# 32-wide attention with the operands of the value product exchanged

## The reference

```python
# layer 0: one shared key and value head
Q = (x @ Wq_w.T + Wq_b).reshape(b, l, NUM_HEADS, HEAD_DIM)
K = x @ Wk_w.T + Wk_b
V = x @ Wv_w.T + Wv_b
scores = jnp.einsum('bqhd,bkd->bhqk', Q, K) * scale
attn = jax.nn.softmax(scores, axis=-1)
out = jnp.einsum('bhqk,bkd->bqhd', attn, V)
# layer 1: keys and values of their own for each head, then an output projection
scores = jnp.einsum('bthd,bshd->bhts', q, k) * softmax_scale
attn = jax.nn.softmax(scores, axis=-1)
ctx = jnp.einsum('bhts,bshd->bthd', attn, v)
```

## Time and profile before

| | |
|---|---|
| median of three runs | 2578.72 us |
| the profiled execution, its time and span | 2575.5 us, 2573.8 us |
| PE busy | 2410.4 us |
| DVE busy | 1743.5 us |
| ACT busy | 1182.5 us |
| 512 weighing records of layer 0, of layer 1 | 116.9 us busy each |

### The profile page before, as it was taken

The page is one execution under the profiler, slowest core; times in us unless marked ns, Lnnn a source line. Parts: engine busy times, 40 slices in busy tenths (PEclk is TensorE's granted clock), DMA queues, the critical chain, the costliest instruction groups (busy, mean ns, idle before and its releaser), DMA issues. The chain is left out here.

```text
span 2573.8 us, 38285 instructions
## 1 busy us (share of the span) xinstructions
PE 2410.4 (94%) x11324; PEld 1771.1 (69%) x11324; DVE 1743.5 (68%) x3696; ACT 1182.5 (46%) x2318; POOL 157.0 (6%) x263
## 2 busy tenths in 40 slices
PE   7899988799999899999996999999999999999679
PEld 5555556677777788555564777777777777776457
DVE  6577877778887654666656666667666666666643
ACT  3477765323333522677723444444444444444221
POOL 0000000100000000000031010101010100000100
PEclk9999999899999999999998999999999999999789
DMA  5622200000000226433102000000000000000101
GB/s 164 196 73 69 71 1 1 1 1 0 0 0 1 83 103 198 112 98 93 41 0 65 2 12 12 16 4 16 4 16 4 16 12 8 12 0 0 43 0 66
DMA packets 71226, 104.10 MB, mean 40 GB/s; under 512 B 14090, under 2 KB 27146, under 8 KB 71018
## 3 DMA queue, kind: packets, MB, share of 16 engines
q1 hardware_dynamic: 71146, 103.08, 13.4%
HBM read 73.16 MB, written 29.88 MB: 40 GB/s over the span
## 5 line engine op out<-in xcount | busy, mean ns | idle before, releaser
L3142 DVE SCALAR_TENSOR_TENSOR x_res<-xa_out_bank,xa_den,x_res 128x512 f32 (+1 forms) x256 | 191.3, 747 | 158.0 <-PE xa_out_bank L2782 158.0
L3051 ACT ACTIVATE xa_pT_hi<-xa_t_bank 128x512 fp32r<-128x512 f32 x256 | 149.5, 597 | 126.0 <-PE xa_t_bank L2919 126.0
L501 DVE TENSOR_REDUCE l1s_mx<-l1s_max_bank 128x1 f32<-128x512 f32 x256 | 156.4, 680 | 68.8 <-PE l1s_max_bank L359 68.8
L3062 ACT ACTIVATE xa_prob<-xa_prob,xa_nmax 128x512 f32<-128x512 f32 x256 | 182.7, 715 | 30.1 <-DVE xa_nmax L3124 30.1
L2782 PE MATMUL xa_out_bank<-xa_o_w,xa_o_hi 128*128 128x512 f32 x512 | 173.9, 421 | 22.3 <-DVE x_res L3142 20.8
L3106 DVE TENSOR_TENSOR xa_pT_lo<-xa_t_bank,xa_pT_hi 128x512 fp32r<-128x512 f32 x256 | 175.6, 686 | 23.1 <-ACT xa_pT_hi L3051 19.0
L501 DVE TENSOR_REDUCE l0s_mx<-l0s_max_bank 128x1 f32<-128x512 f32 x256 | 156.8, 680 | 47.0 <-PE l0s_max_bank L359 46.9
L3124 DVE CUSTOM_DVE_ANT_0 xa_prob<-xa_s_bank,xa_mask_bias 128x512 f32<-128x512 f32 x256 | 171.1, 687 | 20.2 <-PE xa_s_bank L2782 9.6
L2169 DVE SCALAR_TENSOR_TENSOR ffn_yT<-ffn_y,ffn_ysc,ffn_yT 128x512 f32<-128x512 f32 x176 | 129.5, 745 | 46.9 <-PE ffn_y L1915 46.8
L2919 PE MATMUL xa_t_bank<-ident,xa_prob 128*128 128x128 f32 x1024 | 150.6, 275 | 0.0
L2919 PEld LDWEIGHTS xa_t_bank<-ident,xa_prob 128*128 128x128 f32 x1024 | 121.0, 141 | 39.7 <-issue 18.2
(11 more groups left out here) (481 smaller groups left out, 5851.0 us busy)
## 6 DMA issues: line engine op xcount, KB each, us to landing
l0s_q<-l_q SPq DMA_DIRECT2D x96, 128.0 KB, 2.4
l1s_q<-l_q SPq DMA_DIRECT2D x96, 128.0 KB, 3.0
l1s_k<-l_k SPq DMA_DIRECT2D x96, 128.0 KB, 3.1
l0s_k<-l_k SPq DMA_DIRECT2D x96, 64.0 KB, 2.4
x_res<-in_x_dram SPq DMA_DIRECT2D x4, 1024.0 KB, 9.6
l_q<-l_q_hi SPq DMA_DIRECT2D x16, 256.0 KB, 2.6
l_q<-l_q_lo SPq DMA_DIRECT2D x16, 256.0 KB, 3.2
l_q<-l_hi SPq DMA_DIRECT2D x16, 256.0 KB, 2.1
```

The costliest lines, as they stand in the source:

```text
L501: dve.tensor_reduce(self.mx[:, j // QT, j % QT:j % QT + 1], self.max_bank[j % 3][:], AX.X, ALU.max)\
L3051: act.activation(pT_hi[:, kt % (QT - 1), :], t_bank[kt % 2][:], ACT.Copy).then_inc(pT_hi_done, 1)
L3062: act.activation(prob[:, q, :], prob[:, q, :], ACT.Exp, bias=nmax[:, q:q + 1], scale=-1.0, accum_out=den[:, r, 0, q:q + 1]).then_inc(exp_d ...
L3142: dve.scalar_tensor_tensor(xt, out_bank[:], den[:, r, 2, q:q + 1], xt, ALU.mult, ALU.add)\
```

## The change

The two operands of the weighing are exchanged. The probabilities of 128 queries are held (128 columns) and the values with their column of ones are moved (33 columns), one matmul for each key tile, head and query tile: 32 in a pair, where there were 8. The output has queries in partitions, as DVE reads it. ACT's copy, PE's turn, the tile `oT` and the semaphores `oT_ready` and `turned` are gone. Two PSUM banks, before the output's and the turned one's, take the outputs of even and odd pairs. PE waits at the weighing of pair p until DVE has read the output of pair p-2 (`o_read`); DVE's reciprocal waits for the weighing itself. The room that `oT` lent to another weight's scales is a tile of its own.

```diff
         if kt == 0:
             pe.wait_ge(self.v_staged, p + 1)
-            reached(pe, self.oT_ready, p)
+            reached(pe, self.o_read, p - 1)
         pe.wait_ge(self.exp_done, 8 * p + 2 * kt + 2)
         for n in range(2):
-            last = pe.matmul(self.o_bank[self.W * n:self.W * (n + 1), :], self.vs[s % 2][:, kt, n, :],
-                             self.pT[:, n, kt, :], start=(kt == 0), stop=(kt == QT - 1))
+            for q in range(QT):
+                last = pe.matmul(self.o4[s % 2][:, q, n, 0:HD + 1], self.pT[:, n, kt, q * P:(q + 1) * P],
+                                 self.vs[s % 2][:, kt, n, 0:HD + 1],
+                                 start=(kt == 0 and n == 0 and q == 0),
+                                 stop=(kt == QT - 1 and n == 1 and q == QT - 1))
         if kt == QT - 1:
             last.then_inc(self.weighed, 1)
-
-    def turn(self, pe, p):
-
-        pe.wait_ge(self.oT_ready, p + 1)
-        reached(pe, self.o_read, p)
-        for q in range(QT):
-            last = pe.transpose(self.t_bank[:, q * P:(q + 1) * P], self.oT[:, q * P:(q + 1) * P], self.st.ident[:])
-        last.then_inc(self.turned, 1)
...
                 self.score(pe, p, s, k)
-                if k == 4 and not self.early(p, 1):
-                    self.turn(pe, p - 1)
...
-    def take_oT(self, act, p):
-        act.wait_ge(self.weighed, p + 1)
-        reached(act, self.turned, p)
-        act.activation(self.oT[:], self.o_bank[:], ACT.Copy).then_inc(self.oT_ready, 1)
...
-    def invert(self, dve, p):
-        dve.wait_ge(self.turned, p + 1)
-        dve.reciprocal(self.rden[:], self.o4[:, :, :, HD:HD + 1]).then_inc(self.rden_done, 1)
+    def invert(self, dve, p, s):
+        dve.wait_ge(self.weighed, p + 1)
+        reached(dve, self.o_read, p)
+        dve.reciprocal(self.rden[:], self.o4[s % 2][:, :, :, HD:HD + 1]).then_inc(self.rden_done, 1)
...
-        self.o4 = self.t_bank[:].rearrange("p (q n d) -> p q n d", q=QT, n=2)
+        self.o4 = [bank[:].rearrange("p (q n d) -> p q n d", q=QT, n=2) for bank in (self.o_bank, self.t_bank)]
```

More of the change, by code:

```diff
@@ L273, in __init__ @@
             st.sems("maxed", "max_read", "ms_ready", "mrow_turned", "mrow_ready", "scored", "exp_done")
-        self.weighed, self.oT_ready, self.turned, self.o_read, self.max_hi_done, self.rden_done, self.on_done = \
-            st.sems("weighed", "oT_ready", "turned", "o_read", "max_hi_done", "rden_done", "on_done")
+        self.weighed, self.o_read, self.max_hi_done, self.rden_done, self.on_done = st.sems(
+            "weighed", "o_read", "max_hi_done", "rden_done", "on_done")
         self.ks_made, self.vs_cleared, self.vs_made, self.v_staged, self.ms_cleared = \
@@ L290, in __init__ @@
         self.vs = [sb(f"{name}_vs{s}", [P, QT, 2, self.W], F32) for s in range(2)]
-        between("turned")
-        self.oT = sb(f"{name}_oT", [P, S], F32)
+        between("out")
         self.max_bank = [ps(f"{name}_max_bank{g}", [P, S]) for g in range(3)]
@@ L426, in tensor @@
         self.rounds(pe, step)
-        self.turn(pe, self.NP - 1)
     def make_constants(self, pool):
@@ L471, in rows @@
                 .then_inc(self.mrow_ready, 1)
-    def take_oT(self, act, p):
-        act.wait_ge(self.weighed, p + 1)
-        reached(act, self.turned, p)
-        act.activation(self.oT[:], self.o_bank[:], ACT.Copy).then_inc(self.oT_ready, 1)
     def scalar(self, act, beside=None):
         def step(p, s):
-            if not self.early(p, 1):
-                self.take_oT(act, p - 1)
             for k in range(8):
@@ L493, in scalar @@
         self.rounds(act, step)
-        self.take_oT(act, self.NP - 1)
     def reduce(self, dve, p, s, j):
@@ L518, in dest, with normalise @@
             .rearrange("p q (n d) -> p q n d", n=2)
-    def invert(self, dve, p):
-        dve.wait_ge(self.turned, p + 1)
-        dve.reciprocal(self.rden[:], self.o4[:, :, :, HD:HD + 1]).then_inc(self.rden_done, 1)
-    def normalise(self, dve, p):
+    def invert(self, dve, p, s):
+        dve.wait_ge(self.weighed, p + 1)
+        reached(dve, self.o_read, p)
+        dve.reciprocal(self.rden[:], self.o4[s % 2][:, :, :, HD:HD + 1]).then_inc(self.rden_done, 1)
+    def normalise(self, dve, p, s):
         dve.wait_ge(self.rden_done, p + 1)
@@ L527, in normalise @@
             reached(dve, self.on_done, p)
-        dve.tensor_tensor(self.on[:] if self.add else self.dest(p), self.o4[:, :, :, 0:HD],
+        dve.tensor_tensor(self.on[:] if self.add else self.dest(p), self.o4[s % 2][:, :, :, 0:HD],
                           self.rden[:].to_broadcast([P, QT, 2, HD]), ALU.mult).then_inc(self.o_read, 1)
@@ L545, in step @@
             if done:
-                self.invert(dve, p - 1)
+                self.invert(dve, p - 1, s + 1)
             if reducing:
@@ L549, in step @@
             if done:
-                self.normalise(dve, p - 1)
+                self.normalise(dve, p - 1, s + 1)
                 self.add_out(dve, p - 1)
@@ L555, in vector @@
         self.rounds(dve, step)
-        self.invert(dve, self.NP - 1)
-        self.normalise(dve, self.NP - 1)
+        self.invert(dve, self.NP - 1, self.NP - 1)
+        self.normalise(dve, self.NP - 1, self.NP - 1)
         self.add_out(dve, self.NP - 1)
@@ L816, in project_and_attend @@
         wq = att.pT[:, 0, :, :]
-        pk.scale_room = att.on[:].rearrange("p q n d -> p (q n d)").bitcast(F16), att.oT
+        pk.scale_room = att.on[:].rearrange("p q n d -> p (q n d)").bitcast(F16), \
+            sb("l0_scale_rows", [P, 2 * P], F32)
         norm = Norm(st, stack, "l0n", [att.pT[:, 1, s, :] for s in range(QT)])
```

## The result

The kernel after the change takes 3055.93 us (median of four runs, 3051.8 to 3064.19), the kernel before 2578.76 us beside it (2573.06 to 2579.29). The ratio is 1.186, 95% interval 1.1827 to 1.1894: 477 us slower. The forecast was 2932 us with a range up to 3020. The direction, the price of the loads and the fall of the clock came out as forecast; the size of the clock's term did not.

A forecast was written before the change was run, and what follows sets the result against it. DVE's chain of reductions ends a pair's first part, PE alone the second. Swap and clock add 5.56 us a pair, +356 over 64 pairs: 2575.5 + 356 - 2.7 = 2929 us, given as 2932; range 2775 to 3020.

The forecast's parts named there:

- the clock term: Attention pairs: one 6.8 us stretch at 1.2 GHz a pair, raising the added time from +3.43 to +5.56 us a pair.
- The score phase: Part of a pair ahead of its weighing: three matmuls lose 0.2 us each at half clock, counted as +0.2 a pair.
- The weighing: Probabilities times values, at half clock: 33 of a pair's 64 loads take 0.17 us in place of 0.112.
- The dearer case of the prediction: Weighing: a load at 1.2 GHz takes twice 0.112 us, 30 loads in the slow stretch; +6.9 us a pair, 3014 us.
- The load is the price: Weighing at full clock: 64 loads of 128 columns at 0.112 us set its time, 7.17 us in place of 3.59.
- The full-clock sum: Whole kernel with the clock kept at 1.00: +219 us over 64 pairs less 2.7 us, 2792 us.
- The swap's step: Weighing with operands exchanged, at full clock: +3.43 us a pair, +219 us over 64 pairs.
- The gaps count as missing columns: Weighing: load gaps between short streams lower the granted clock, although PE does not wait; forecast chance 0.62.
- the clock stays: Rival, on the weighing: loads count as work, so the price is the loads alone, 2792 us; chance 0.27.
- Removed turns: 0: Four transposes of the previous output, 0.44 us of a pair, go without gain; bounds 0 and 28 us over 64 pairs.
- The tail: Behind the last pair of each stage: 1.35 us between weighing and reciprocal go, twice, -2.7 us.
- The waits: 0, with two banks: PE's wait at a weighing for DVE's read of two pairs before never bites; DVE's moved reciprocal wait also costs 0.

The follow-up runs named there:

- the first experiment: The changed kernel with 64 moved columns in place of 33, loads and records the same in number: 2790.95 us, ratio 1.0839.

## Why the prediction was wrong

**What failed: the size of the clock term, and in it the score phase.** The step reads: "Let each pair have one stretch at 1.2 GHz as long as the one from 98.10, 6.8 us, beginning halfway through the weighing: 31 loads at 0.112 (3.5 us), 33 at 0.17 (5.6), then 1.2 us of the score phase in which three matmuls lose 0.2 each, most of it before DVE's chain is the later: +0.2". The score phase is the part of a pair ahead of its weighing. The term was 356 - 219 = 137 us, 2.1 a pair; it measured 265 us, 4.14 a pair. Its two parts, against the kernel with 64 columns, in which the clock stayed at 1.00:

*The score phase: +0.2 a pair forecast, some 1.7 measured, 95 of the missing 128 us.* The weighing accounts for 157 of the 265 us (next point), so 108 are left for the score phases, where 13 were forecast. PE's timeline, after, beside the lines from 200.09 to 211.51 above:

```profile
193.54 0.77 PE L358 MATMUL l0s_max_bank<-l0s_k,l0s_q 96*128 96x512 f32 x1
...
199.62 0.40 PE L358 MATMUL l0s_max_bank<-l0s_k,l0s_q 96*128 96x512 f32 x1
...
217.91 1.36 PE L390 MATMUL l0s_t_bank<-l0s_vs,l0s_pT 128*128 128x33 f32 x11
```

One score phase lasts from 193.54 to 200.33, 6.79 us, the next from 211.51 to 217.91, 6.40 us, where it was 4.52 at full clock. The windows above have the clock back at 199.60 and at 216.60, so it was low for 6.1 and 5.1 us of them and not for 1.2. Over both stages the granted clock is at 0.50 for 329 us in weighings and for 332 us in score phases. The error is the stretch: 6.8 us was the shortest of the three lengths in the window of three pairs (6.8, 10.3 and 13.6 us, 64% of the time, where 6.8 in 13.78 is 49%), and it was laid almost wholly into the weighing. In these stages the clock came back only inside a score phase.

*The weighing: +1.9 a pair forecast, 2.45 measured.* It is 624.5 us busy against 467.4 with 64 columns, so +157, where 33 x (0.17 - 0.112) x 64 = 122 were forecast. Here two errors partly cancel. A load takes 0.213 us at 0.50 and not 0.17; the 0.17 came from the distance between two loads at 99.90 and 100.07 in the earlier trace rows, of which the first had waited, and such a distance shows when a load could begin and not what a run of loads costs. But by the intervals above some 22 loads a pair ran slow and not 33.

The dearer case of the prediction, a load at twice 0.112, comes to 3014 us, near the 3055.93 measured, and that nearness is luck: it gives the weighing 3.5 + 6.8 + 0.3 = 10.6 us, where the mean is 9.6, and lets the score phase lose nothing. The upper end of the range was drawn from it, with the shortest stretch, so the measured time lies outside.

The Trainium skill, "TensorE: Matmul & The Clock Gate", "LDWEIGHTS (loading the stationary operand)", gives a load as its columns over 1.2, in ns, with no clock in it; for 128 columns that is an estimate of 107. This case agrees within 5% at full clock (0.112 us) and not at half, where the load took 0.213. By the page's formula the loads would cost the same in slow stretches; the measurement decides against it.

**What held.**

- *The load is the price.* 64 x 0.112 = 7.17 us was forecast for the weighing at full clock, and 7.11 measured with 64 moved columns. The full-clock sum of 2792 us was met by 2791. Twice the columns at the same loads cost nothing, and halved loads brought the weighing to 3.85. The swap's step of +3.43 us a pair measured +3.38 (216/64, with the two tails in it).
- *The gaps count as missing columns.* The choice between two readings of the rows fell right: with 33 columns for each load the clock fell although PE was busy throughout, with 64 it did not fall. The prediction had no row for this and said so; the first experiment shows it. The rival "the clock stays", to which I gave 0.27, describes exactly the kernel with 64 columns.
- *Removed turns: 0.* Three of four removed changed the time by +0.14%. The reason given, that DVE's reductions end the phase, shows in the waits of 0.30 us. In slow stretches of the changed kernel PE ends the phase instead (below).
- *The tail.* In the changed kernel DVE's last reciprocal of the stage comes right behind the last products, where 1.35 us lay between the earlier trace rows. The timeline after:

```profile
610.11 1.68 PE L390 MATMUL l0s_t_bank<-l0s_vs,l0s_pT 128*128 128x33 f32 x7
611.83 0.21 DVE L506 RECIPROCAL l0s_rden<-l0s_t_bank 128x8 f32<-128x8 f32 x1 [8.37 <-PE l0s_t_bank L390]
```

- *The waits: 0, with two banks.* PE is busy in all of the three-pair window. The experiment with one bank shows what the second one is for, in the form with 64 columns: 82 us of wait, and with the clock 474 us.

Three expected signs held only in part. The clock digits came down to 6 and 7, not 7 or 8. DVE is idle for (47.80 - 19.54)/3 = 9.4 us of a pair, not 7. And the rows of maxima stand behind a reduction where the clock stayed at 1.00 (in the kernel with 64 columns their load waits 0.30 us for DVE), but not in slow stretches, where DVE itself waits for PE between reductions (0.16 us, and 9.85 before the first). DVE's timeline, after:

```profile
212.32 0.69 DVE L484 TENSOR_REDUCE l0s_mx<-l0s_max_bank 128x1 f32<-128x512 f32 x1 [9.85 <-PE l0s_max_bank L358]
213.18 0.69 DVE L484 TENSOR_REDUCE l0s_mx<-l0s_max_bank 128x1 f32<-128x512 f32 x1 [0.16 <-PE l0s_max_bank L358]
```

These reductions start 0.86 apart, the pace of two 512-column matmuls at 0.43. At full clock they were 0.60 apart.

## What to carry to other kernels

Price a swap of held and moved operand by the loads that it makes, not by the columns it saves: here the weighing took twice the time on PE at full clock (7.11 against 3.59 us), because each load of 128 columns (0.112 us) stood beside a stream of 33. When PE is busy but mostly loading, price the clock too. In the slow part take the PE durations at 1.8 to 1.9 times their full-clock value (0.43 against 0.24 us for a 512-column matmul, 0.213 against 0.112 for a load), and do not end the slow part with the thin one: here half of the slow time lay in the dense phase behind it. A wait of a microsecond in such a loop is to be priced the same way; here the clock that it cost was more than four times the wait.

## What the runs showed of the hardware that was not expected

- A run of weight loads scales with the granted clock like matmuls do: 0.112 us at 1.00, 0.213 at 0.50, for 128 columns of f32.
- The clock, lost in the thin phase of a pair, came back 6.1 and 5.1 us into the dense phase behind it; half of the time at 0.50 (332 of 661 us) lay in dense phases.
- Loads into the two column halves of the array run side by side: 128 records of 64 weight columns in 3.85 us, against 64 of 128 in 7.11.
- Moving more columns made a kernel faster by 265 us, through the clock alone.
- A wait of 1.3 us a pair on average cost 474 us over 64 pairs, 82 of them as waiting, the rest through the clock.
- A loop body with 128 short matmuls a pair left PE with gaps of 3 to 5 us where the loop jumps; written out there were none. With 256 a pair, PE stood still in the middle of its weighings though its loop was written out (158 records in 1.55 us, then 2.09 us of nothing), mostly 253 or 254 matmuls after the last such gap.
